# Cross-attention in rounds of one sequence, four head groups on row and column tiles of the array

## The chip, the cores and the metric

The kernel is one program on one core of a Trainium2 chip. Its engines are TensorE (PE, with its weight loads shown apart as PEld), VectorE (DVE), ScalarE (ACT) and GpSimd (POOL); SyncE (SP) issues transfers. The time is the device time of the program in microseconds, the median of several runs; lower is better. Beside it stands one profiled execution, from which every duration below is read.

## The reference, cut to what matters

The kernel computes six blocks one after the other: a cross-attention, a self-attention with rotary positions, a mixture-of-experts block, an LSTM with attention, four Mamba layers and a last expert block. The change lies in the first and its seam to the second. With 8 sequences of 32 queries, 512 context rows, 16 heads of width 8:

```python
def _L0_xattn_ref(x, y, padding_mask, Wq, bq, Wkv, bkv, qn_w, qn_b, kn_w, kn_b, Wo, bo):
    ...
    q = (x @ Wq.T + bq).reshape(b, s1, h, d)
    kv = (y @ Wkv.T + bkv).reshape(b, s2, 2, h, d)
    k, v = (kv[:, :, 0], kv[:, :, 1])
    q = _ln(q, qn_w, qn_b) * scale
    k = _ln(k, kn_w, kn_b)
    attn = jnp.einsum('bihd,bjhd->bhij', q, k)
    attn = jnp.where(padding_mask[:, None, None, :], attn, -jnp.inf)
    p = jax.nn.softmax(attn, axis=-1)
    ctx = jnp.einsum('bhij,bjhd->bihd', p, v).reshape(b, s1, c)
    out = ctx @ Wo.T + bo
    return out
...
x = x + _L0_xattn_ref(_layernorm(x, axis=-1), ctx_1024, mask_BxS2_bk0, ...)
x = x + _L0_attn_ref(_layernorm(x, axis=-1), ...)
```

## The kernel before

Each engine has its own program, and the order of work on an engine is the order in which the program is written; engines wait for one another at semaphores. All data of this stage are float32, and the compiler turns one float32 matmul into two instructions on PE.

**Projections.** Keys, queries and values of all 8 sequences are projected and the keys and queries normalised over each head (`k_proj`, `k_var`, `k_square`, `k_hat`, L325 to L357 and L500 to L524). Partition p of `kT` and of the queries holds feature p, so that 32 partitions hold a group of 4 heads. DVE spreads the queries into `qblk` (L810 to L818): for each of 16 heads one instruction multiplies all 128 partitions by a mask that leaves the 8 partitions of that head. POOL has set `qblk` to zero before (L381).

**Softmax steps.** There are 32 steps, i = 4b + g, for sequence b and group g of 4 heads. A step has 128 rows (4 heads by 32 queries) and 512 columns (context). PE: `x_scores` (L1369, one matmul over all 128 partitions of `kT`, of which the mask leaves 32 at work), into `bank[i % 2]`. DVE: `x_max` adds the mask and takes the row maximum (L839), then negates it (L841). ACT: `x_exp` (L531), which also gives the row sum. DVE: `x_norm`, the reciprocal of the sum (L847) and the multiplication by it (L850). PE: `x_transpose`, four 128x128 transposes (L1377). ACT: `x_copy_pt` copies them out of PSUM (L538). PE: `x_pv`, four matmuls with 32 columns of values as weights (L1386), output on the 32 partitions of group g. Every tile between these is double-buffered (slots i % 2 of `T`). After the four groups of a sequence DVE picks each head's own part out of the product (`x_heads`, L858 and L861).

PE's loop runs scores of step i, transposes of step i - 2, product of step i - 3. DVE's loop runs `x_max(i)`, `x_norm(i - 1)`, every fourth time `x_heads`, and in between takes maxima that a later block needs: `l_size` (L866) over the 8 parts of the context in steps 0 to 7 and over three parts of the weights `lw` at step 12. ACT runs `x_exp(i)`, `x_copy_pt(i - 2)`.

**Around the steps.** Ahead of the steps DVE computes `wmean` (L828, L829) from the self-attention's weights; POOL then subtracts it from them (L405) and scales parts of `lw` (L411). After the steps DVE reduces the maxima to `ltop` (L882, L883), POOL reduces these over partitions (L415) for a later block, and only then adds a bias for the self-attention (L418) and sets `qblk` to zero for it (L420). Meanwhile the output projection (L1399), the residual (L889) and layernorm 1 (L762 to L788) run, and the self-attention begins: PE `a_proj` (L1414), `a_var` (L1422), `a_rot` (L1429); ACT `a_square`, `a_rstd` (L553 to L560); DVE `a_z0` (L906), `a_rope` (L916, L918, L922); POOL L426; 8 turns m of these, then scores L1451, whose softmax DVE begins at L942, and the product L1473.

Of the kernel before, what the change touches and what calls it, by code (L numbers as in the profile page):

```python
# [36 lines left out]
XG = 4  # L37
# [90 lines left out]
def build(nc, arr, out, upto=99):  # L128

    with ExitStack() as ctx:  # L130
# [127 lines left out]
        def slot(n, i):  # L258
# [120 lines left out]
        def _(pool):  # L379
            step = Steps(pool, sem["pool_step"])  # L380
            pool.memset(qblk[:, :, :, :, :], 0.0).then_inc(sem["mask_ready"], 1)  # L381

            pool.wait_ge(sem["d_mask"], 16)
            pool.tensor_scalar(maskb[:, :], mask8[:, :], -MASKED, MASKED, ALU.mult, ALU.add) \
# [93 lines left out]
        def _(act):  # L478
# [47 lines left out]
            def x_exp(i):  # L526

                act.wait_ge(sem["x_max"], i + 1)
                if i >= 2:
                    act.wait_ge(sem["x_norm"], i - 1)  # L530
                act.activation(T[:, 2 + i % 2, :], T[:, i % 2, :], ACT.Exp, bias=xneg[:, i:i + 1],  # L531
                               accum_out=xz[:, i:i + 1]).then_inc(sem["x_exp"], 1)

            def x_copy_pt(i):
                act.wait_ge(sem["x_tr"], i + 1)
                if i >= 2:
                    act.wait_ge(sem["x_pv"], i - 1)
# [216 lines left out]
        def _(dve):  # L754
# [55 lines left out]
            def q_blocks(first):  # L810

                if first == 0:
                    dve.wait_ge(sem["k_done"], 1)
                    dve.wait_ge(sem["mask_ready"], 1)
                for h in (first, first + 1):
                    ins = dve.tensor_scalar(qblk[:, h // 4, :, h % 4, :], T[:, 10, 0:TOK].rearrange("p (b s) -> p b s", b=B),  # L816
                                            cst[:, C_HM16 + h:C_HM16 + h + 1], None, ALU.mult)
                ins.then_inc(sem["qblk_ready"], 1)  # L818

            for s in range(1 + B):  # L820
# [3 lines left out]
                if s >= 1:  # L824
                    q_blocks(2 * (s - 1))

            dve.wait_ge(sem["d_attn"], 32)
            step(dve.tensor_reduce(wmean[:, :], wqkv[:, 0:2 * AH * AD].rearrange("p (h d) -> p h d", d=AD), AX, ALU.add))  # L828
            dve.tensor_scalar(wmean[:, :], wmean[:, :], 1.0 / AD, None, ALU.mult).then_inc(sem["a_wmean"], 1)  # L829

            def x_max(i):

                b = i // XG
                if i == 0:
                    dve.wait_ge(sem["mask_ready"], 2)
                dve.wait_ge(sem["x_score"], i + 1)
                if i >= 2:
                    dve.wait_ge(sem["x_exp"], i - 1)
                step(dve.tensor_tensor_reduce(T[:, i % 2, :], bank[i % 2][:, :], maskb[:, b * SK:(b + 1) * SK],  # L839
                                              1.0, FLOOR, ALU.add, ALU.max, xmax[:, i:i + 1]))  # L840
                dve.tensor_scalar(xneg[:, i:i + 1], xmax[:, i:i + 1], -1.0, None, ALU.mult) \  # L841
                   .then_inc(sem["x_max"], 1)

            def x_norm(i):
# [3 lines left out]
                if i >= 2:  # L848
                    dve.wait_ge(sem["x_tr"], i - 1)
# [1070 lines left out]
```

## Time and profile before

| what | time, us |
|---|---|
| median of 3 runs | 739.34 (737.47 to 740.51) |
| the profiled execution | 740.16 |
| its span, first to last instruction | 738.3 |
| projections of the cross-attention | 13.4 to 36.8 |
| softmax steps, first scores to last `x_heads` | 40.44 to 125.2 |
| output projection and layernorm 1 | 125.3 to 130.1 |
| self-attention, 8 turns and after | 130.2 to 186.9 |
| mixture of experts, LSTM, Mamba, last block | 186.9 to 738.3 |

The first section of the profile page gives each engine's busy time, the second the busy share in 40 slices of 18.5 us (a digit is tenths; the row PEclk is the granted clock of TensorE in tenths of full speed). The other views group instructions by source line, list them in order of time, or give sums over stretches of time. A releaser behind an arrow is what ended the idle time ahead of an instruction.

### The profile page before, as it was taken

The page shows a single profiled execution, that of the slowest core. Times are in us where ns is not written, and L with a number is a line of the kernel's source. Part 1 is how long each engine was busy: PE and PEld are TensorE (multiplying, and loading weights), DVE is VectorE, ACT ScalarE, POOL GpSimd, SP SyncE. Part 2 cuts the span into 40 slices and gives each one's busy share as a digit, 9 for nine tenths or more (in the row PEclk, how much of TensorE's full clock was granted, in tenths as well). Part 3 has the DMA queues.
Part 4 walks back from the last instruction along what each step waited for, and adds up shares of the span by engine and source line. Part 5 has one row for each costly group of instructions (what it writes and reads, how often), then busy time and mean ns, then how long its engine had stood idle before and what let it go on. Part 6 is the DMA issues. An engine that isn't in the chain of part 4 may idle for free.

```text
span 738.3 us, 21781 instructions
## 1 busy us (share of the span) xinstructions
PE 618.2 (84%) x8501; PEld 476.5 (65%) x8501; DVE 498.4 (68%) x1962; ACT 306.1 (41%) x859; POOL 144.8 (20%) x177
## 2 busy tenths in 40 slices
PE   4969997876889758999899998997689888988866
PEld 3536665434678558888888888886466556655634
DVE  1697665477453467777777777774287888878883
ACT  2935453433365543333333333333445445544511
POOL 3330000420800000000000000000543564346500
PEclk9999999887799855555555555555599999999997
DMA  9700000000100200000000000000000000000000
GB/s 344 321 1 1 1 1 2 1 1 2 41 1 1 66 22 3 0 0 0 0 0 0 0 0 0 0 0 1 0 1 1 0 1 1 1 0 1 0 1 7
DMA packets 6057, 15.26 MB, mean 21 GB/s; under 512 B 2640, under 2 KB 3288, under 8 KB 5504
## 3 DMA queue, kind: packets, MB, share of 16 engines
q1 hardware_dynamic: 5296, 11.19, 4.1%
q10 hardware_dynamic: 720, 3.55, 1.2%
q8 instruction: 24, 0.39, 0.2%
q14 instruction: 17, 0.14, 0.1%
HBM read 14.60 MB, written 0.13 MB: 20 GB/s over the span
## 4 chain that ended last, share of the span: by engine, by line
PE 49%; DVE 30%; ACT 11%; issue 8%; DMA 1%; POOL 1%; DVEq 0%; SPq 0%; ACTq 0%
PE bank L1659 9%; PE bank L1732 7%; PE bank L1568 6%; PE bank L1386 4%; PE bank L1369 4%; ACT esp L661 3%; PE bank L1519 2%; DVE ssum L1122 2%; DVE T L1192 2%; ACT a L647 2%; ACT e L663 2%; PE bank L1377 2%; PE bank L1506 2%; DVE rz L1159 2%; DVE zs L1157 2%
## 5 line engine op out<-in xcount | busy, mean ns | idle before, releaser
L1568 PE MATMUL bank<-esp,qblk 128*128 128x1 f16 (+1 forms) x2048 | 66.6, 166 | 0.7 <-ACT esp L661 0.7
L1568 PE MATMUL bank<-hsp,kT 128*128 128x2 f16 x2048 | 63.6, 166 | 2.5 <-DVE hsp L1150 1.7
L1568 PEld LDWEIGHTS bank<-hsp,kT 128*128 128x128 f16 x2048 | 60.0, 104 | 3.5 <-DVE hsp L1147 1.7
L1568 PEld LDWEIGHTS bank<-esp,qblk 128*128 128x128 f16 x2048 | 61.3, 104 | 1.3 <-ACT esp L661 1.1
L647 ACT ACTIVATE a<-opre 128x4 f32<-128x4 f32 x64 | 13.1, 205 | 115.8 <-DVE opre L1110 115.8
L455 POOL MEMSET ctxT<- 128x128 f32 x1 | 0.3, 312 | 306.2 <-DVE xres L1166 306.2
L1192 DVE SCALAR_TENSOR_TENSOR T<-bank,bct,T 128x256 f32<-128x256 f32 x112 | 46.4, 475 | 1.3 <-PE bank L1745 1.3
L1179 DVE TENSOR_TENSOR_SCAN qblk<-ctxT,bank 128x512 f32<-128x512 f32 x32 | 37.6, 1208 | 13.5 <-PE bank L1732 13.1
L1568 PE MATMUL bank<-asp,lsp 128*128 128x4 f16 x768 | 30.7, 168 | 16.4 <-DVE asp L1112 16.4
L1568 PEld LDWEIGHTS bank<-asp,lsp 128*128 128x128 f16 x768 | 25.4, 105 | 27.9 <-DVE asp L1112 27.7
L1179 DVE TENSOR_TENSOR_SCAN w<-kT,bank 128x512 f32<-128x512 f32 x32 | 37.5, 1207 | 8.2 <-PE bank L1732 8.2
L531 ACT ACTIVATE T<-T,xneg 128x512 f32<-128x512 f32 x32 | 23.1, 722 | 42.1 <-DVE xneg L841 42.1
L1369 PE MATMUL bank<-kT,qblk 128*128 128x512 f32 x64 | 37.1, 668 | 3.6 <-DVE qblk L816 3.6
L655 ACT ACTIVATE gact<-bank,lgate 128x16 f32<-128x16 f32 x64 | 17.5, 274 | 45.6 <-PE bank L1568 45.6
L1732 PE MATMUL bank<-maskb,T 128*128 128x512 f32 x64 | 35.9, 685 | 0.5 <-ACT T L725 0.5
L1732 PE MATMUL bank<-w,T 128*128 128x512 f32 x64 | 34.9, 660 | 1.0 <-DVE w L1179 1.0
L839 DVE CUSTOM_DVE_ANT_0 T<-bank,maskb 128x512 f32<-128x512 f32 x32 | 22.1, 690 | 19.9 <-PE bank L1369 19.9
L1568 PE MATMUL bank<-hsp,lsp 128*128 128x4 f16 x984 | 35.4, 166 | 0.0
L1386 PE MATMUL bank<-T,vx 128*32 128x128 f32 x256 | 33.6, 276 | 0.2
L1568 PE MATMUL bank<-gx,T 128*128 (+1 forms) x198 | 27.7, 190 | 6.5 <-DVE gx L1091 6.5
L1568 PEld LDWEIGHTS bank<-hsp,lsp 128*128 128x128 f16 x984 | 32.0, 105 | 0.0
L473 POOL TENSOR_TENSOR kT<-T,aneg 128x496 f32<-128x496 f32 x32 | 31.3, 1015 | 3.3 <-DVE T L1249 3.3
(327 smaller groups left out, 1471.1 us busy)
## 6 DMA issues: line engine op xcount, KB each, us to landing
w<-in_w_dram SPq DMA_DIRECT2D x2, 2048.0 KB
ctxT<-in_ctxT_dram SPq DMA_DIRECT2D x8, 256.0 KB, 12.9
wqkv<-in_qkvT_dram ACTq DMA_DIRECT2D x1, 1536.0 KB, 11.7
w<-in_mw_dram SPq DMA_DIRECT2D x1, 1024.0 KB, 5.1
lw<-in_lw_dram SPq DMA_DIRECT2D x1, 960.0 KB, 19.8
rows<-in_rows_dram ACTq DMA_DIRECT2D x1, 772.0 KB, 7.9
wqkv<-in_fw_dram SPq DMA_DIRECT2D x1, 532.0 KB, 3.3
T<-in_mask_dram ACTq DMA_DIRECT2D x1, 512.0 KB, 5.8
```

The lines of the kernel that those rows point to most:

```text
L473: pool.tensor_tensor(tile(c, i), pat(delta, [[0, NG], [S, BT], [1, S - 1]], ch * P + 1), pat(aneg[:, :], [[1, NG], [0, BT], [0, S - 1]], ( ...
L531: act.activation(T[:, 2 + i % 2, :], T[:, i % 2, :], ACT.Exp, bias=xneg[:, i:i + 1], accum_out=xz[:, i:i + 1]).then_inc(sem["x_exp"], 1)
L647: act.activation(a32[:, g, :], opre[:, g, :], ACT.Tanh).then_inc(sem["at_32"], 1)
L661: act.activation(esp[:, g, 0, :], ssum[:, g, :], ACT.Exp, scale=lexp[:, :]) \
L839: step(dve.tensor_tensor_reduce(T[:, i % 2, :], bank[i % 2][:, :], maskb[:, b * SK:(b + 1) * SK], 1.0, FLOOR, ALU.add, ALU.max, xmax[:, i: ...
L1179: dve.tensor_tensor_scan(out=hid[q % 2][:, at], data0=decay[q % 2][:, at], data1=bank[i % 4][:, :], initial=0.0, op0=ALU.mult, op1=ALU.add ...
L1192: ins = dve.scalar_tensor_tensor(out=cacc[n % 2], in0=hT, scalar=c_n, in1=cacc[n % 2], op0=ALU.mult, op1=ALU.add)
L1369: pe.matmul(bank[i % 2][:, :], qblk[:, g, b, :, :], kT[:, b * SK:(b + 1) * SK], start=True, stop=True).then_inc(sem["x_score"], 1)
L1386: ins = pe.matmul(bank[4 + b % 2][32 * g:32 * g + 32, 0:P], vx[:, b * KC + c, 32 * g:32 * g + 32], T[:, 6 + i % 2, c * P:(c + 1) * P], sta ...
L1568: return pe.matmul(out, lhsT, rhs, start=start, stop=stop, skip_group_check=True)
L1659: return pe.matmul(out, lhsT, rhs, start=start, stop=stop, skip_group_check=True)
L1732: pe.matmul(bank[i % 4][:, :], duT[s][:, ch * P:(ch + 1) * P], diagb[s][:, ng * 512:(ng + 1) * 512], start=True, stop=True).then_inc(sem[" ...
```

## The change

**PE, rows.** The queries are spread into 4 blocks instead of 16: block h carries head h of every group, on that group's 32 partitions (`q_block`, mask `C_HM`, four instructions; the scale is now a constant with a minus sign). Scores of group g are then a matmul over the 32 partitions of the group alone, and the four groups of a sequence are issued one after the other into banks 0 to 3 (`x_scores(b)`), after all four `x_max` of the sequence before.

**PE, columns.** `x_pv(b)` runs once for a sequence, with the four groups inside the loop over the parts of the context, so that neighbouring matmuls have different output partitions. It waits for all four copies of the sequence.

**PE, order.** Round b is scores of sequence b, product of sequence b - 2, sixteen transposes of sequence b - 1.

**DVE.** The scores come out negated; so the maximum becomes a minimum that is at once the bias of the exponential, and the negation (L841) with the wait ahead of it goes. The exponential and the division are written in place; there are six slots for them (`XR`) and eight for the transposed probabilities. `wmean` is computed in round 0, after the third division. The `l_size` of the context move into the 8 turns of the self-attention, those of `lw` and the reduction to `ltop` behind these turns.

**ACT.** `x_copy_pt` runs four steps behind `x_exp`, instead of two.

**POOL.** The first zeroing of `qblk` goes. The reduction over partitions moves from ahead of the self-attention's bias to behind its 8 turns.

Semaphores of the last block are replaced by ones that exist already (`f_gate`, `f_h`), with the counts adapted.

The diff, cut to this:

```diff
-            pool.memset(qblk[:, :, :, :, :], 0.0).then_inc(sem["mask_ready"], 1)
...
-            pool.wait_ge(sem["l_stat"], 1)
-            pool.partition_all_reduce(lall[:, :], ltop[:, :], P, REDUCE.max).then_inc(sem["l_max"], 1)
-
             pool.wait_ge(sem["x_res"], 1)
             pool.tensor_tensor(xbias[:, :, :], xres[:, :, :], pat(r("projb"), [[0, NJ], [1, D]]), ALU.add) \
                 .then_inc(sem["xb_ready"], 1)
...
+
+            pool.wait_ge(sem["l_stat"], 1)
+            pool.partition_all_reduce(lall[:, :], ltop[:, :], P, REDUCE.max).then_inc(sem["l_max"], 1)
...
-                if i >= 2:
-                    act.wait_ge(sem["x_norm"], i - 1)
-                act.activation(T[:, 2 + i % 2, :], T[:, i % 2, :], ACT.Exp, bias=xneg[:, i:i + 1],
+                act.activation(x_soft(i), x_soft(i), ACT.Exp, scale=-1.0, bias=xneg[:, i:i + 1],
                                accum_out=xz[:, i:i + 1]).then_inc(sem["x_exp"], 1)
...
+            for i in range((B + 1) * XG):
                 if i < B * XG:
                     x_exp(i)
-                if i >= 2:
-                    x_copy_pt(i - 2)
+                if i >= XG:
+                    x_copy_pt(i - XG)
...
+                dve.tensor_scalar(qblk[:, 0, :, h, :], T[:, 10, 0:TOK].rearrange("p (b s) -> p b s", b=B),
+                                  cst[:, C_HM + h:C_HM + h + 1], -XD ** -0.5, ALU.mult, ALU.mult) \
+                   .then_inc(sem["qblk_ready"], 1)
...
-                step(dve.tensor_tensor_reduce(T[:, i % 2, :], bank[i % 2][:, :], maskb[:, b * SK:(b + 1) * SK],
-                                              1.0, FLOOR, ALU.add, ALU.max, xmax[:, i:i + 1]))
-                dve.tensor_scalar(xneg[:, i:i + 1], xmax[:, i:i + 1], -1.0, None, ALU.mult) \
-                   .then_inc(sem["x_max"], 1)
+                if i >= XR:
+                    dve.wait_ge(sem["x_tr"], i - XR + 1)
+                dve.tensor_tensor_reduce(x_soft(i), bank[g][:, :], maskb[:, b * SK:(b + 1) * SK],
+                                         1.0, -FLOOR, ALU.add, ALU.min, xneg[:, i:i + 1]).then_inc(sem["x_max"], 1)
...
+            for b in range(B + 2):
+                for g in range(XG):
+                    i = b * XG + g
+                    if i < B * XG:
+                        x_max(i)
+                    if 1 <= i <= B * XG:
+                        x_norm(i - 1)
+                if b == 0:
+                    dve.wait_ge(sem["d_attn"], 32)
+                    step(dve.tensor_reduce(wmean[:, :], wqkv[:, 0:2 * AH * AD].rearrange("p (h d) -> p h d", d=AD), AX, ALU.add))
+                    dve.tensor_scalar(wmean[:, :], wmean[:, :], 1.0 / AD, None, ALU.mult).then_inc(sem["a_wmean"], 1)
+                if b >= 2:
+                    x_heads(b - 2)
...
                 if m >= 1:
                     a_rope(m - 1)
+                if m < B:
+                    l_size(lmax[:, m:m + 1], ctxT[:, m * SK:(m + 1) * SK])
+            dve.wait_ge(sem["l_w"], 4)
+            for k, (at, end) in enumerate(((14, 15), (13, 14), (4, 13))):
+                l_size(lmax[:, B + k:B + k + 1], lw[:, at * D:end * D])
...
+                for g in range(XG):
+                    own = slice(32 * g, 32 * g + 32)
+                    pe.matmul(bank[g][:, :], qblk[own, 0, b, :, :], kT[own, b * SK:(b + 1) * SK],
+                              start=True, stop=True).then_inc(sem["x_score"], 1)
...
                 for c in range(KC):
-                    ins = pe.matmul(bank[4 + b % 2][32 * g:32 * g + 32, 0:P], vx[:, b * KC + c, 32 * g:32 * g + 32],
-                                    T[:, 6 + i % 2, c * P:(c + 1) * P], start=(c == 0), stop=(c == KC - 1))
+                    for g in range(XG):
+                        ins = pe.matmul(bank[6 + b % 2][32 * g:32 * g + 32, 0:P], vx[:, b * KC + c, 32 * g:32 * g + 32],
+                                        x_probT(b * XG + g)[:, c * P:(c + 1) * P], start=(c == 0), stop=(c == KC - 1))
...
+            for b in range(B + 2):
+                if b < B:
+                    x_scores(b)
+                if b >= 2:
+                    x_pv(b - 2)
+                if 1 <= b <= B:
+                    for g in range(XG):
+                        x_transpose((b - 1) * XG + g)
```

PE at the start of the softmax steps, before: scores (L1369), transposes (L1377) and products (L1386) in steps.

```order
L1369 MATMUL bank<-kT,qblk 128x512 x3
L1377 MATMUL bank<-cst,T 128x128 x4
L1369 MATMUL bank<-kT,qblk 128x512
L1377 MATMUL bank<-cst,T 128x128 x4
L1386 MATMUL bank<-T,vx 32x128 x4
```

The same place after the change, to the end of round 2:

```order
L1369 MATMUL bank<-kT,qblk 128x512 x8
L1377 MATMUL bank<-cst,T 128x128 x16
L1369 MATMUL bank<-kT,qblk 128x512 x4
L1386 MATMUL bank<-T,vx 32x128 x16
L1377 MATMUL bank<-cst,T 128x128 x16
```

The number of matmuls is the same; they now stand in fours and sixteens.

POOL from the subtraction of `wmean` on, before (the rows "ISA" without operands are set-up instructions):

```order
L405 TENSOR_TENSOR wqkv<-wqkv,wmean 128x2048
L411 TENSOR_SCALAR lw<-lw 128x128
L411 TENSOR_SCALAR lw<-lw 128x384
L411 TENSOR_SCALAR lw<-lw 128x128
L413 MEMSET expo 128x1
L415 ISA
L415 ISA lall<-ltop 128x4
L418 ISA
L418 TENSOR_TENSOR xbias<-xres,rows 128x256
L420 MEMSET qblk 128x4096
L426 TENSOR_SCALAR T<-T,vec 128x512 x8
```

And after (L434 is the reduction over partitions):

```order
L412 TENSOR_TENSOR wqkv<-wqkv,wmean 128x2048
L418 TENSOR_SCALAR lw<-lw 128x128
L418 TENSOR_SCALAR lw<-lw 128x384
L418 TENSOR_SCALAR lw<-lw 128x128
L420 MEMSET expo 128x1
L422 TENSOR_TENSOR xbias<-xres,rows 128x256
L424 MEMSET qblk 128x4096
L430 TENSOR_SCALAR T<-T,vec 128x512 x8
L434 ISA
L434 ISA lall<-ltop 128x4
```

The bias and the zeroing no longer stand behind the reduction.

## Rows read from the trace of the kernel before

**Rows 1.** Sums by stretch: us, busy time by engine (instructions), PEclk, DMA share, GB/s

```profile
80.00:100.00 20.00, 20.00 (x115) 12.85 (x114) 12.56 (x45) 10.51 (x25) 0.00 (x0) 1.00 0.00 1
```

**Rows 2.** One step in order of time, all engines: start, length, instruction [idle before]

```profile
114.60 0.15 DVE L847 RECIPROCAL xrz<-xz 128x1 f32<-128x1 f32 x1
...
114.78 0.49 DVE L850 TENSOR_SCALAR T<-T,xrz 128x512 f32<-128x512 f32 x1
...
115.11 1.13 PE L1369 MATMUL bank<-kT,qblk 128*128 128x512 f32 x2
...
116.07 0.60 PE L1377 MATMUL bank<-cst,T 128*128 128x128 f32 x4
...
116.28 0.69 DVE L839 CUSTOM_DVE_ANT_0 T<-bank,maskb 128x512 f32<-128x512 f32 x1 [1.00 <-PE bank L1369]
...
116.60 1.06 PE L1386 MATMUL bank<-T,vx 128*32 128x128 f32 x8
```

**Rows 3.** PE in order of time: products of the self-attention, two column tiles

```profile
176.41 1.97 PE L1473 MATMUL bank<-qblk,vx 128*64 128x128 f32 x32 [1.55 <-DVE qblk L963]
```

**Rows 4.** In order of time: scores of the self-attention, tiles of 64 rows by 32 columns

```profile
163.74 2.34 PE L1451 MATMUL bank<-kT 64*32 64x32 f32 x204 [1.58 <-DVE kT L922]
```

**Rows 5.** In order of time: start of the softmax steps

```profile
40.30 2.27 DVE L828 TENSOR_REDUCE wmean<-wqkv 128x32 f32<-128x2048 f32 x1
...
40.44 4.52 PE L1369 MATMUL bank<-kT,qblk 128*128 128x512 f32 x6 [3.62 <-DVE qblk L816]
...
42.87 3.62 POOL L405 TENSOR_TENSOR wqkv<-wqkv,wmean 128x2048 f32<-128x2048 f32 x1 [1.91 <-DVE wmean L829]
...
45.14 1.63 DVE L850 TENSOR_SCALAR T<-T,xrz 128x512 f32<-128x512 f32 x1
```

**Rows 6.** In order of time: end of the softmax steps, layernorm 1

```profile
124.46 0.29 DVE L858 TENSOR_TENSOR T<-bank,cst 128x128 f32<-128x128 f32 x1 [3.01 <-PE bank L1386]
124.79 0.37 DVE L861 TENSOR_REDUCE oT<-T 128x32 f32<-128x128 f32 x1
...
126.56 0.42 DVE L889 TENSOR_TENSOR xres<-xbias,bank 128x256 f32<-128x256 f32 x1 [0.87 <-PE bank L1399]
...
128.38 0.61 DVE L783 TENSOR_SCALAR xn<-xres,mv,rs 128x128 f32<-128x128 f32 x2 [0.60 <-ACT rs L491]
```

**Rows 7.** POOL in order of time, 125 to 138 us

```profile
133.16 0.71 POOL L418 TENSOR_TENSOR xbias<-xres,rows 128x256 f32<-128x256 f32 x1 [7.21 <-issue]
133.83 3.50 POOL L420 MEMSET qblk<- 128x4096 f32 x1
```

**Rows 8.** In order of time: layernorm 0 beside POOL

```profile
7.14 3.60 POOL L384 TENSOR_SCALAR maskb<-T 128x4096 bf16<-128x4096 uint8 x1 [2.89 <-DMA T<-in_mask_dram]
...
10.01 1.06 DVE L783 TENSOR_SCALAR xn<-x_in,mv,rs 128x128 f32<-128x128 f32 x2 [5.26 <-ACT rs L491]
```

**Rows 9.** DVE in order of time: a turn of the self-attention, and behind the turns

```profile
149.23 0.75 DVE L906 SCALAR_TENSOR_TENSOR T<-bank,vec,T 128x512 f32<-128x512 f32 x1 [0.83 <-ACT T L560]
...
155.46 0.75 DVE L906 SCALAR_TENSOR_TENSOR T<-bank,vec,T 128x512 f32<-128x512 f32 x1 [0.82 <-ACT T L560]
...
165.41 0.76 DVE L942 SCALAR_TENSOR_TENSOR T<-bank,cst 128x256 f32<-128x256 f32 x2 [1.72 <-PE bank L1451]
```

**Rows 10.** Groups by line, `l_size` of the context: count, busy us, mean ns, idle before

```profile
L866 DVE TENSOR_REDUCE lmax<-ctxT 128x1 f32<-128x512 f32 x8 | 5.4, 677 | 0.0
```

**Rows 11.** DVE in order of time: `l_size` of `lw`

```profile
72.96 1.73 DVE L866 TENSOR_REDUCE lmax<-lw 128x1 f32<-128x128 f32 x3
```

**Rows 12.** Sums by stretch, columns as in Rows 1, around changes of the clock

```profile
124.00:128.00 4.00, 1.14 (x8) 0.68 (x6) 2.31 (x10) 0.18 (x1) 0.39 (x1) 1.00 0.00 0
...
132.00:136.00 4.00, 4.00 (x9) 2.44 (x8) 0.00 (x0) 1.46 (x3) 2.84 (x2) 0.50 0.00 0
136.00:140.00 4.00, 2.91 (x10) 1.50 (x9) 1.69 (x3) 2.86 (x5) 2.12 (x3) 1.00 0.00 0
...
176.00:180.00 4.00, 2.41 (x36) 2.20 (x37) 3.80 (x8) 1.09 (x2) 0.00 (x0) 1.00 0.00 0
```

More of the change, by code:

```diff
@@ L535, in x_copy_pt @@
                 act.wait_ge(sem["x_tr"], i + 1)
-                if i >= 2:
-                    act.wait_ge(sem["x_pv"], i - 1)
-                act.activation(T[:, 6 + i % 2, :], bank[2 + i % 2][:, :], ACT.Copy).then_inc(sem["x_pt"], 1)
-            for i in range(B * XG + 2):
+                if i >= 2 * XG:
+                    act.wait_ge(sem["x_pv"], i // XG - 1)
+                act.activation(x_probT(i), bank[4 + i % 2][:, :], ACT.Copy).then_inc(sem["x_pt"], 1)
+            for i in range((B + 1) * XG):
                 if i < B * XG:
                     x_exp(i)
-                if i >= 2:
-                    x_copy_pt(i - 2)
+                if i >= XG:
+                    x_copy_pt(i - XG)
             ln_rstd(1)
@@ L808, in v_evac, with q_block @@
                 dve.tensor_copy(pat(vx[:, b * KC, :], [[1, SK]]), bank[4 + b % 2][:, :]).then_inc(sem["v_evac"], 1)
-            def q_blocks(first):
-                if first == 0:
+            def q_block(h):
+                if h == 0:
                     dve.wait_ge(sem["k_done"], 1)
[L814 to L818, printed above, removed]
+                dve.tensor_scalar(qblk[:, 0, :, h, :], T[:, 10, 0:TOK].rearrange("p (b s) -> p b s", b=B),
+                                  cst[:, C_HM + h:C_HM + h + 1], -XD ** -0.5, ALU.mult, ALU.mult) \
+                   .then_inc(sem["qblk_ready"], 1)
             for s in range(1 + B):
@@ L866, in l_size @@
                 step.mark(dve.tensor_reduce(to, of, AX, ALU.max, apply_absolute_value=True))
-            for i in range(B * XG + 4):
-                if i < B * XG:
-                    x_max(i)
-                if 1 <= i <= B * XG:
-                    x_norm(i - 1)
-                if i >= 4 and (i - 4) % XG == XG - 1:
-                    x_heads((i - 4) // XG)
-                if i < B:
-                    l_size(lmax[:, i:i + 1], ctxT[:, i * SK:(i + 1) * SK])
-                if i == 12:
-                    dve.wait_ge(sem["l_w"], 4)
-                    for k, (at, end) in enumerate(((14, 15), (13, 14), (4, 13))):
-                        l_size(lmax[:, B + k:B + k + 1], lw[:, at * D:end * D])
-            step.sync()
-            step(dve.tensor_reduce(ltop[:, 0:1], lmax[:, 0:B], AX, ALU.max))
-            dve.tensor_copy(ltop[:, 1:4], lmax[:, B:B + 3]).then_inc(sem["l_stat"], 1)
+            for b in range(B + 2):
[11 more added lines that the diff above has]
+                    x_heads(b - 2)
             dve.wait_ge(sem["x_oT"], B)
@@ L929, in _ @@
                     a_rope(m - 1)
+                if m < B:
[3 more added lines that the diff above has]
+                l_size(lmax[:, B + k:B + k + 1], lw[:, at * D:end * D])
+            step.sync()
+            step(dve.tensor_reduce(ltop[:, 0:1], lmax[:, 0:B], AX, ALU.max))
+            dve.tensor_copy(ltop[:, 1:4], lmax[:, B:B + 3]).then_inc(sem["l_stat"], 1)
             dve.wait_ge(sem["a_rope"], 8)
@@ L1366, in x_scores @@
                     pe.wait_ge(sem["k_rstd"], 1 + B)
-                if i >= 2:
-                    pe.wait_ge(sem["x_max"], i - 1)
-                pe.matmul(bank[i % 2][:, :], qblk[:, g, b, :, :], kT[:, b * SK:(b + 1) * SK],
-                          start=True, stop=True).then_inc(sem["x_score"], 1)
+                else:
+                    pe.wait_ge(sem["x_max"], XG * b)
+                for g in range(XG):
+                    own = slice(32 * g, 32 * g + 32)
+                    pe.matmul(bank[g][:, :], qblk[own, 0, b, :, :], kT[own, b * SK:(b + 1) * SK],
+                              start=True, stop=True).then_inc(sem["x_score"], 1)
             def x_transpose(i):
```

66 lines of the change are left out of this document (27 added, 39 removed).

## The prediction

> **What bounds the kernel now.** I read the sums by stretch first. In the middle of the softmax steps PE is busy 20.00 of 20.00 us at the full clock, DVE 12.56, ACT 10.51 [rows 1]. Then one step in order of time [rows 2]: scores begin at 115.11, transposes at 116.07, the product at 116.60, and `x_max` waits 1.00 us for the scores. The spans of 1.13, 0.60 and 1.06 us overlap at their ends. The product's 8 instructions of 128 columns start 109 ns apart, 0.85 us in all; at that pace the scores' two of 512 also stream 0.85, and the transposes' four 0.43. Two changes of form a step leave some 0.2 us each. That is 2.5 us. 32 steps from the first scores at 40.44 [rows 5] to the last `x_heads` at 125.16 [rows 6] make 84.7 us, all of it on the path, since the self-attention needs their result.
>
> DVE's own step, without waits, is the second thing to see. From its begin to the next instruction's, `x_max` takes 0.68 (116.28 with 0.69 long), the reciprocal 0.19 (114.60 to 114.78), the multiplication 0.41 of its 0.49. ACT's 10.51 us in 20 are 1.3 a step, 1.2 where its instructions follow one another closely.
>
> **The scores and the product.** *Do tiles run side by side?* For column tiles the trace shows it. The self-attention's products use two column tiles: 32 instructions of 128 columns in 1.97 us [rows 3], 62 ns each. The same length on one column tile costs 8 in 1.06 us, 109 ns apart [rows 2]. So two tiles run at once. Its scores, on 64 rows by 32 columns, start 204 instructions in 2.34 us [rows 4], 11.5 ns each, where 32 columns stream for 27 ns (a quarter of 109); so more than two tiles can be at work. Four row tiles of 32 with 512 columns are in no row. Bounds: the four scores take 4 x 0.85 = 3.4 us a round if they don't overlap, 0.85 if they do wholly. I take 0.85, by the nearest rows, 3 and 4. The Trainium skill (TensorE: Matmul & The Clock Gate, Part 3) gives 3.07x for four row tiles at 512 columns. That would make 1.1 us of the scores, and 0.26 us more in each of seven rounds, an estimate of 1.8 us by that page; no row here has the form.
>
> *PE's round* at the full clock is then 0.85 + 0.87 + 4 x 0.44 = 3.5 us of streaming and 0.6 for three changes of form, against 10 before. PE no longer bounds.
>
> *DVE's round* is what is late next: 4 x (0.68 + 0.19 + 0.41) = 5.1, and `x_heads` 0.6 [rows 6]. The negation (0.15 and its wait) is gone. Scores of the next sequence start only after the fourth `x_max` and need 1.13 us to the first result [rows 2]; one division (0.6) and `x_heads` (0.6) stand in this gap, so 0.1 to 0.4 us stays open. I followed the waits of the three programs with these durations and get **6.1 us a round**, 1.52 a step. ACT's 4 x 1.22 = 4.9 fits in.
>
> *The ends.* First scores at 40.3 (they wait for POOL's last part of `kT`, not for `qblk`); the clock there is low (three matmuls in 4.52 us [rows 5]), so the first `x_max` begins at 42.4, as before. Round 0 has `wmean`, 2.45 us with its scaling [rows 5], for which before the first scores were a cover; here the gap and the missing `x_heads` cover half: 7.3 us. Round 1 has POOL's subtraction. In the trace the multiplication at 45.14 takes 1.63 in place of 0.49 and ends as POOL's L405 does [rows 5]. Now that 3.6 us instruction begins 0.8 us ahead of the fourth division: a stall of 2.4 us, 8.1 for the round. Five more rounds of 6.0 to 6.1. From the last round's first `x_max` to the last `x_heads`: four steps (4.5), the rest of divisions and transposes, with copies one behind the other (5.3), product and heads (2.1): 11.9. Sum 42.1 + 7.3 + 8.1 + 30.3 + 11.9 = **99.7 at the full clock**.
>
> *The clock.* After 124 to 128, with PE busy 1.14 of 4.00 us, it fell from 2.4 to 1.2 GHz; in 132 to 136 PE was busy all the time at 0.50, and from 136 it had 1.00 [rows 12]. Here PE idles some 4 us after the first scores, so rounds 0 and 1 run at 1.2 GHz. There PE has 7 us of streaming and 0.6 of changes; the round comes to 7.95 us. It is then nearly always busy, which should bring 2.4 GHz back. I take two to three rounds at 7.95: **the steps end at 104**, 21.2 us sooner. Bounds are 99.7 and 114.7 (all rounds low).
>
> **What is moved.** *POOL, reduction over partitions.* POOL stood 7.21 us after it [rows 7], so bias and zeroing came at 133.16. Now both start as soon as the residual is there, 0.05 us after L889. The bias takes 0.7, the zeroing 3.5, till 4.25 us after L889; layernorm's multiplication (two instructions, 0.61) is due 1.40 us after it (128.38 against 126.98) [rows 6]. Where POOL held on, DVE's same line took 1.06 at 10.01 and ended 0.33 after POOL's L384 [rows 8], and L850 waited likewise [rows 5]. POOL read and wrote in both; whether a zeroing, which only writes, holds DVE up is in no row. Bounds 0 and 4.25 + 0.28 - 1.40 - 0.3 = **+2.9**; I take 2.9, as DVE writes too and both nearest rows show a full stop. DVE idled before L906 for 7 us while PE projected, but that wait begins behind this multiplication, so nothing covers it. The Trainium skill (SBUF — State Buffer, "Who interferes with whom") says that a GpSimd instruction and such a VectorE multiplication exclude each other for their whole length; by that rule the sum stands, and with no hold it would be 720.6. The reduction itself now runs behind the turns, where POOL idles until the self-attention ends: nothing.
>
> *`l_size`, context.* 8 x 0.68 [rows 10], 0.60 from begin to begin. Before they lay in DVE's idle time. In the turns DVE idles 0.83 of 6.2 us per two turns [rows 9]; two of them ask 1.2, so 0.4 a pair stays, and one chain is delayed at once: **+2.0** over 8 turns (bounds 0 and 4.8).
>
> *`l_size`, lw, and ltop.* 1.73 [rows 11] and 0.4, in DVE's wait of 1.72 for L1451 [rows 9]: **+0.4**. Taking ltop out of the end of the steps gives 0.2 back.
>
> *First zeroing, 12 fewer instructions for `qblk`:* nothing. POOL waits for the mask by transfer anyway [rows 8], and the projections are PE's.
>
> **Sum.** -21.2 + 2.9 + 2.0 + 0.4 - 0.2 = -16.1. The profiled execution, 740.16, becomes 724.1. The median of the runs is 0.8 lower, so 723.3; I say **723.5**.
>
> **Rivals.**
> (a) *Clock back at once, zeroing free.* Steps end at 101, and the 2.9 falls away: **717**. For it: PE's low rounds are dense. Against: rows 5 and 8.
> (b) *Low clock throughout.* With 7.6 of 7.95 us PE is not quite without a break, and once high it has only 57% to do, with four short transposes late in a round. In 176 to 180, with 2.41 of 4.00 us busy, the clock stayed up [rows 12], which speaks against. Steps end at 114.7: **734**.
> (c) *Row tiles one after the other.* Scores take 3.4 us, PE's round 6.7 plus waits, 8.1 by the same reckoning; steps end at 112 to 118: **731 to 737**. This is the change not doing what it says. For it: only column tiles are shown; against: rows 4 mix two halves of the rows.
> (d) *Slower.* (c) with the clock held low: scores 6.8, round 13.1 us, steps end at 148, 23 later than now; with the 5 us moved, **767**. It costs more than now from about 9 us a round (now 4 x 2.48 = 9.9, but the moved 5 us and the longer ends count against it). PE would be busy all the time, as in 132 to 136, after which the clock rose; hence it is unlikely.
>
> **How the numbers follow.** Forecast 0.50 (719 to 728), (a) 0.13, (b) 0.15, (c) 0.14, (d) 0.04, 0.04 for seams I don't see. The range leaves out (d), half of (a)'s lower and (c)'s upper end: 715.5 to 736. Half a percent, what a measurement can tell from no change, is 3.7 us: faster below 735.6. Chances: 0.88 faster, 0.06 the same, 0.06 slower.
>
> **What would show it.** Scores: eight instructions of 512 columns in about 1.1 us, one end; if 3.5, (c). DVE: from round 2 on begins of `x_max` 1.3 us apart, with one gap a round, and little idle time between; PE idle a third. PEclk 0.5 in the stretch 44 to 58 and 1.0 after; 0.5 throughout is (b). The fourth division near 3 us long. Layernorm 1's multiplication 3.5 us in place of 0.61, beside POOL's zeroing; 0.6 refutes it. Turns of the self-attention 3.3 us in place of 3.1. I am wrong altogether if the steps end later than 120.

## The result, and the profile after

The changed kernel takes **720.61 us** (median; runs 719.57 to 720.94) against 738.40 for the kernel before on the same chip (737.39 to 740.51). The ratio is 0.9753, with a 95% interval of 0.9726 to 0.978: faster by 2.5%, where 723.5 had been forecast in a range of 715.5 to 736. The profiled execution took 740.16 before and takes 720.94 now, with a span of 719.1.

The page of the changed kernel, its first two sections and the group of the transposes (line, engine, operation, tiles; busy us and mean ns; idle time before and its releaser):

```profile
PE 578.0 (80%) x8501; PEld 450.8 (63%) x8501; DVE 491.9 (68%) x1918; ACT 304.4 (42%) x859; POOL 139.8 (19%) x176
...
PEclk9978988978999555555555555555699999999996
...
L1377 PE MATMUL bank<-cst,T 128*128 128x128 f32 x128 | 21.0, 303 | 10.0 <-ACT T L543 9.8
```

The page hardly shows the change: it lies in the third to tenth of 40 slices. So I put the milestones of both traces beside one another (us from the span's start, or differences of such times):

| from the trace | before | after | difference |
|---|---|---|---|
| last `x_heads` ends | 125.16 | 102.24 | -22.92 |
| from there to layernorm 1's multiplication | 3.22 | 3.08 | -0.14 |
| that multiplication, two instructions | 0.61 | 3.00 | +2.39 |
| its end to the first `a_proj` | 1.22 | 1.32 | +0.10 |
| the eight turns of the self-attention | 33.47 | 34.37 | +0.90 |
| last turn to its softmax | 1.73 | 1.97 | +0.24 |
| softmax to the end of the self-attention | 21.53 | 21.29 | -0.24 |
| from there to the span's end | 551.40 | 551.86 | +0.46 |
| span | 738.34 | 719.14 | -19.2 |

Some 22.9 us came out up to the end of the softmax steps and some 3.7 were given back behind them. The last row but one is work that none of the experiments below touches; over the twelve traces of this document it takes 549.1 to 551.9 us, and this is how far chance alone moves a single trace. Sums by stretch of the changed kernel (us; busy time and instructions of PE, PEld, DVE, ACT, POOL; PEclk), to be read beside [rows 1]:

```profile
44.00:58.00 14.00, 7.54 (x32) 3.74 (x32) 12.36 (x27) 6.81 (x18) 4.84 (x5) 0.62 0.00 0
60.00:80.00 20.00, 15.39 (x184) 9.90 (x180) 17.71 (x61) 16.31 (x40) 0.00 (x0) 0.99 0.01 2
80.00:100.00 20.00, 14.53 (x164) 9.79 (x164) 14.41 (x48) 14.77 (x35) 0.00 (x0) 0.91 0.00 1
```

In 60 to 80 PE is busy 15.39 of 20 us, no longer 20.00, and DVE 17.71. DVE is the bound now. (PE's busy time still looks high because the spans of single matmuls, 273 ns for 128 columns, run on past the next one's start, 109 ns later.) The seam between two rounds, in order of time, all engines:

```profile
75.37 1.14 PE L1369 MATMUL bank<-kT,qblk 32*128 32x512 f32 x8
75.43 0.49 DVE L845 TENSOR_SCALAR T<-T,xrz 128x512 f32<-128x512 f32 x1
...
75.83 0.28 DVE L852 TENSOR_TENSOR T<-bank,cst 128x128 f32<-128x128 f32 x1
...
76.53 0.69 DVE L838 CUSTOM_DVE_ANT_0 T<-bank,maskb 128x512 f32<-128x512 f32 x1
76.91 0.81 PEld L1386 LDWEIGHTS bank<-T,vx 128*32 128x32 f32 x32 [1.23 <-ACT T L543]
76.91 1.08 PE L1386 MATMUL bank<-T,vx 128*32 128x128 f32 x32 [0.40 <-ACT T L543]
...
77.15 0.16 DVE L844 RECIPROCAL xrz<-xz 128x1 f32<-128x1 f32 x1
...
79.94 0.16 DVE L844 RECIPROCAL xrz<-xz 128x1 f32<-128x1 f32 x1 [0.30 <-ACT T L536]
```

The scores of four head groups take 1.14 us, as long as those of one group took before (1.13 [rows 2]); the products of four take 1.08 where one took 1.06. Rounds, from one sequence's first `x_max` to the next one's, are 7.00, 9.28, 6.51, 5.92, 5.91, 5.92, 5.92 us; before, four steps took 9.93.

### The profile page after: what moved, and what is told of

Read it like the earlier page. It is cut to its first block, busy times and chain, and to the rows that moved or that the text cites. A ratio compares the mean times of both kernels' runs of the same rounds, so it can differ in the third digit from the quotient of the medians.

```text
span 719.1 us, 21665 instructions
## 1 busy us (share of the span) xinstructions
PE 578.0 (80%) x8501; PEld 450.8 (63%) x8501; DVE 491.9 (68%) x1918; ACT 304.4 (42%) x859; POOL 139.8 (19%) x176
## 4 chain that ended last, share of the span: by engine, by line
PE 41%; DVE 33%; ACT 14%; issue 9%; DMA 1%; DVEq 1%; POOL 0%; SPq 0%; ACTq 0%; POOLq 0%
PE bank L1660 9%; PE bank L1733 7%; PE bank L1569 6%; ACT esp L666 3%; PE bank L1520 2%; ACT T L536 2%; DVE ssum L1121 2%; ACT a L652 2%; DVE T L1191 2%; ACT e L668 2%; PE bank L1507 2%; DVE rz L1158 2%; DVE zs L1156 2%; DVE asp L1111 2%; DVE opre L1097 2%
## 5 line engine op out<-in xcount | busy, mean ns | idle before, releaser
L660 ACT ACTIVATE gact<-bank,lgate 128x16 f32<-128x16 f32 x64 | 17.5, 274 | 45.6 <-PE bank L1569 45.6
L480 POOL TENSOR_TENSOR ctxT<-T,aneg 128x496 f32<-128x496 f32 x32 | 31.2, 1012 | 3.1 <-DVE T L1248 3.1
L1377 PE MATMUL bank<-cst,T 128*128 128x128 f32 x128 | 21.0, 303 | 10.0 <-ACT T L543 9.8
L1121 DVE TENSOR_REDUCE ssum<-bank 128x16 f32<-128x64 f32 x64 | 14.4, 225 | 18.6 <-PE bank L1569 18.6
## 6 DMA issues: line engine op xcount, KB each, us to landing
wqkv<-in_qkvT_dram ACTq DMA_DIRECT2D x1, 1536.0 KB, 11.9
```

The lines of the kernel that those rows point to most:

```text
L480: pool.tensor_tensor(tile(c, i), pat(delta, [[0, NG], [S, BT], [1, S - 1]], ch * P + 1), pat(aneg[:, :], [[1, NG], [0, BT], [0, S - 1]], ( ...
L660: act.activation(gact[:, g, :], bank[GATES[g]][:, 0:4 * BH], ACT.Tanh, scale=lgate[:, :]) \
L1121: dve.tensor_reduce(ssum[:, g, :], pat(bank[1][:, 0:1], [[1, BH * KC], [BANK, 2], [BH * KC, 2]]), mybir.AxisListType.XY, ALU.add).then_inc ...
L1377: ins = pe.transpose(bank[4 + i % 2][:, c * P:(c + 1) * P], x_soft(i)[:, c * P:(c + 1) * P], ident)
```

## Experiments

Each edit is made to the changed kernel. Ratios are to the kernel before, run beside it on the same chip. Differences to the changed kernel are between medians taken apart, of which it has two, 720.61 and 719.56 us; the trace of each run is of one execution.

**Rows undone, columns kept** (`e1_rows_undone`).

```diff
-                dve.tensor_scalar(qblk[:, 0, :, h, :], ..., cst[:, C_HM + h:C_HM + h + 1], -XD ** -0.5, ...)
+                for h in (first, first + 1):
+                    ins = dve.tensor_scalar(qblk[:, h // 4, :, h % 4, :], ..., cst[:, C_HM16 + h:C_HM16 + h + 1], -1.0, ...)
...
-                    pe.matmul(bank[g][:, :], qblk[own, 0, b, :, :], kT[own, b * SK:(b + 1) * SK],
+                    pe.matmul(bank[g][:, :], qblk[:, g, b, :, :], kT[:, b * SK:(b + 1) * SK],
```

> The changed kernel with its scores again over all 128 partitions (16 query blocks, one matmul per group); everything else as changed. Theory (tiles running side by side is what freed TensorE): the four scores of a round stream 3.4 us in place of 0.85 us, the round grows from 5.9 to about 8.1 us at the full clock, the steps end 12 to 17 us later, the time is 733 to 738 us. Rival (the gain is from fewer changes of form on TensorE and a shorter VectorE step; tiles matter little): under 724 us.

731.91 us, ratio 0.9903 (0.9887 to 0.992), just under the range expected. PE in order of time, in a middle round:

```profile
84.50 3.70 PE L1369 MATMUL bank<-kT,qblk 128*128 128x512 f32 x8
88.13 1.08 PE L1386 MATMUL bank<-T,vx 128*32 128x128 f32 x32
```

The same eight instructions of 512 columns take 3.70 us in place of 1.14. In the trace of single instructions they start 429 to 534 ns apart; in the changed kernel four start 7 ns apart and the other four 534 ns later. So four row tiles run wholly side by side, and this is worth 2.1 us a round (8.01 in place of 5.92). The steps end at 117.33 in place of 102.24, 15.1 us later and so within the 12 to 17 expected; of the 15.1, 4.1 come back behind the steps, 2.7 of them in that last part of the kernel, which the edit doesn't touch.

**Columns undone, rows kept** (`e2_cols_undone`).

```diff
-                for c in range(KC):
-                    for g in range(XG):
+                for g in range(XG):
+                    for c in range(KC):
```

> The changed kernel with only the order of the product's 16 matmuls changed: group outside, part of the context inside, so that neighbours share their output partitions. Theory: the product takes 3.4 us a round in place of 0.87 us, and it stands ahead of the transposes, so the round grows from 5.9 to about 8.6 us; the steps end 18 to 22 us later, 738 to 743 us. Rival: order does not matter, because TensorE reaches ahead to another column tile by itself: 721 us, unchanged.

729.04 us, ratio 0.9867 (0.9846 to 0.9888): between what the two theories gave. PE in order of time:

```profile
87.08 1.14 PE L1369 MATMUL bank<-kT,qblk 32*128 32x512 f32 x8
88.61 2.46 PE L1386 MATMUL bank<-T,vx 128*32 128x128 f32 x32 [0.39 <-ACT T L543]
```

The instructions and their tiles are those of the changed kernel, only their order differs, and 1.08 us became 2.46. The single starts show why it isn't the 3.4 us of one after the other: of each group of eight the last four start in pairs with the first four of the next group, 6 to 31 ns ahead of them (which start belongs to which group follows from the order of the program and the pace of 109 ns; the trace doesn't name the tile). So PE begins a second tile four instructions early, and gets no further ahead. The 32 starts take 2.19 us with never more than two tiles at work; in the changed kernel they come in fours, 7 ns apart, and take 0.81 us. The round is 7.30 us, 1.38 longer, exactly the product's growth. With a product of 3.4 us, one after the other, the eight of them would take 8 x 0.94 = 7.5 us more, and the time would be near 736.5; most of the distance to the range expected is this overlap.

**Both undone, new order kept** (`e3_both_undone`), the two edits together.

> Both undone: scores over 128 partitions and the product group by group, in the new rounds, with the new VectorE and ScalarE parts. Theory: 31 to 37 us over the changed kernel, 751 to 758 us, so slower than the kernel before, because the rounds alone give TensorE 9 us of streaming one behind the other with waits in between. Rival (rounds and the shorter VectorE step carry a good part of the gain): at or below 735 us, faster than the kernel before.

744.77 us (740.68 to 745.96), ratio 1.0084 (1.0062 to 1.0105), slower than the kernel before by 0.8%. The trace is of the quickest of the four runs, 4.1 us under the median; where the others spend these 4 us isn't shown. PE in order of time, then the sums of 80 to 100 us:

```profile
87.48 3.70 PE L1369 MATMUL bank<-kT,qblk 128*128 128x512 f32 x8
91.12 2.46 PE L1386 MATMUL bank<-T,vx 128*32 128x128 f32 x32
```

```profile
80.00:100.00 20.00, 17.95 (x117) 11.13 (x115) 12.22 (x41) 10.76 (x26) 0.00 (x0) 1.00 0.00 1
```

The round is 9.39 us: 3.47 more than in the changed kernel, and rows and columns alone gave 2.09 and 1.38, together 3.47. From first scores to last `x_heads` it takes 85.3 us, and before 84.7. A steady round is 0.54 us shorter than the four steps of before (9.39 against 9.93), but from the last round's first `x_max` to the last `x_heads` it takes 18.6 us, where the same stretch took 13.9 before. So the order in rounds, the wider buffers and the dropped negation together bring nothing over the whole of the steps; the net gain there comes from tiles that run side by side. The time is 6 us under the range expected, about what the product's overlap of two tiles spares (7.5 us by the reckoning above).

**The cost of the zeroing** (`e4_zero_after_ln`; POOL waits ahead of it until layernorm 1 has written its result).

```diff
+            pool.wait_ge(sem["ln_xn"], 2)
             pool.memset(qblk[:, :, :, :, :], 0.0).then_inc(sem["a_zero"], 1)
```

> The changed kernel with one wait added on GpSimd: the zeroing of qblk starts only after layernorm 1 has written its result. Theory (the zeroing, though it only writes, holds the multiplication of layernorm 1 up): that line falls from 3.00 to 0.61 us and the time by 2.4 us, to 718.2 us. Rival (the multiplication is slow for another reason, or the 2.4 us are covered by the low clock of the first projections): 720.6 us, unchanged.

716.24 us, ratio 0.9702 (0.9681 to 0.9722): 4.4 under the changed kernel, more than the 2.4 us that the trace shows of it. The two medians had not been taken side by side, so both kernels ran once more, on one chip.

> The changed kernel once more, beside the next one on the same chip, to part the effect of the zeroing from where the clock's changes happen to fall. Theory (the zeroing costs 2.4 us; what the earlier comparison showed beyond that, 2 us, came from the clock, which rose sooner there and did not fall again in the steps): 720.6 us within 1.5 us.

> The changed kernel with the zeroing of qblk behind layernorm 1, once more. Theory: 2.4 us under the kernel beside it, 718.2 us, with single runs from 714 to 719 by the clock. Rival (the wait saves 4.4 us by itself): 716.2 us with the kernel beside it at 720.6 us.

719.56 us (718.08 to 721.82) and 715.32 (714.93 to 718.53), ratios 0.9744 (0.972 to 0.9767) and 0.9693 (0.9667 to 0.9718). The difference of the medians is 4.2 again, that of the means 3.6: nearer the rival's 4.4 than the theory's 2.4. In order of time, with the zeroing moved:

```profile
106.06 0.60 DVE L789 TENSOR_SCALAR xn<-xres,mv,rs 128x128 f32<-128x128 f32 x2 [0.60 <-ACT rs L499]
...
106.72 3.51 POOL L425 MEMSET qblk<- 128x4096 f32 x1 [1.26 <-DVE xn L789]
```

The multiplication is back at 0.60 us: 2.4 are shown to be the zeroing's. From the last `x_heads` to the end of the self-attention the traces of this pair differ by 3.23 (64.26 and 61.03). The 0.8 beyond the multiplication goes with the clock: 0.25 ahead of the first `a_proj`, 0.4 in the turns, 0.2 behind them. Sums by stretch of the changed kernel's second run, PEclk before the last two numbers:

```profile
104.00:108.00 4.00, 0.00 (x0) 0.00 (x0) 3.33 (x7) 0.50 (x2) 3.68 (x2) 0.89 0.14 8
108.00:112.00 4.00, 2.69 (x7) 1.97 (x8) 1.07 (x3) 0.00 (x0) 0.49 (x1) 0.50 0.00 0
112.00:116.00 4.00, 4.00 (x13) 2.65 (x11) 0.00 (x0) 2.35 (x4) 0.00 (x0) 0.75 0.00 0
```

And of the kernel with the zeroing moved:

```profile
104.00:108.00 4.00, 0.80 (x5) 0.47 (x4) 2.18 (x8) 0.50 (x2) 2.00 (x2) 0.94 0.14 8
108.00:112.00 4.00, 4.00 (x11) 2.87 (x12) 0.00 (x0) 1.19 (x2) 2.23 (x1) 0.64 0.00 0
112.00:116.00 4.00, 2.70 (x9) 1.42 (x8) 2.06 (x4) 3.01 (x5) 0.69 (x1) 1.00 0.01 2
```

PE idles while DVE is held up, and the projections behind that begin at 1.2 GHz (0.50) in the one and come back to 2.4 sooner in the other. The last 1 us of the 4.2 is in no row that I can name: runs of one kernel differ by 3.7 us, and go with the mean clock (718.08 at 0.749, 721.82 at 0.737, the same kernel), and the last part of the kernel, which no experiment touches, ranges over 2.8 us in the traces, so it may be chance. It stays open. That the clock stayed up in the steps, which the theory named for the rest, isn't needed for it: in this pair it fell in both (93.5 to 100.3 and 93.8 to 100.7).

**`wmean` ahead of the steps** (`e5_wmean_first`; reduction and scaling moved from round 0 to before the first `x_max`).

```diff
+            dve.wait_ge(sem["d_attn"], 32)
+            step(dve.tensor_reduce(wmean[:, :], ...))
+            dve.tensor_scalar(wmean[:, :], wmean[:, :], 1.0 / AD, None, ALU.mult).then_inc(sem["a_wmean"], 1)
...
-                if b == 0:
-                    dve.wait_ge(sem["d_attn"], 32)
-                    step(dve.tensor_reduce(wmean[:, :], ...))
-                    ...
```

> The changed kernel with wmean computed ahead of the first x_max again, where VectorE waits 3 us for scores. Theory: 2.3 us leave round 0 (of which up to 0.6 come back as a gap before the scores of the next round), and GpSimd's subtraction starts 8 us sooner and holds one division up by 1.5 us in place of 2.8; steps 3 to 4 us shorter, time 717 us. Rival (wmean was covered by TensorE at its low clock in round 0): 720.6 us.

717.77 us, ratio 0.9699 (0.9668 to 0.973). DVE in order of time; the reduction fills the wait for the first scores again, and POOL's subtraction, which it releases, now holds up an earlier division (1.75 us in place of 0.49):

```profile
39.72 2.27 DVE L831 TENSOR_REDUCE wmean<-wqkv 128x32 f32<-128x2048 f32 x1
...
42.65 0.69 DVE L842 CUSTOM_DVE_ANT_0 T<-bank,maskb 128x512 f32<-128x512 f32 x1 [0.45 <-PE bank L1369]
...
44.43 1.75 DVE L849 TENSOR_SCALAR T<-T,xrz 128x512 f32<-128x512 f32 x1
...
50.16 0.69 DVE L842 CUSTOM_DVE_ANT_0 T<-bank,maskb 128x512 f32<-128x512 f32 x1 [1.56 <-PE bank L1369]
```

The steps are 2.1 us shorter, not the 3 to 4 expected, and the rival was half right. Round 0 isn't shorter at all (7.51 in place of 7.00): the held-up division stands in it now, and where `wmean` had been, DVE waits 1.56 us for scores that PE delivers at 1.2 GHz. The gain is in rounds 1 and 2 (6.48 and 6.12 in place of 9.28 and 6.51).

**The subtraction behind the divisions** (`e9_sub_after_norms`).

```diff
+            pool.wait_ge(sem["x_norm"], B * XG)
             pool.tensor_tensor(wqk, wqk, pat(wmean[:, :], [[1, 2 * AH], [0, AD]]), ALU.subtract) \
```

> The changed kernel with one wait added on GpSimd: the subtraction of wmean from the weights starts only after the last of the 32 divisions. Theory (the division of 3.27 us in round 1 is held up by this subtraction): all 32 divisions take 0.49 us, the steps are 2.8 us shorter, and with no long idle time of TensorE in round 1 the clock may rise one round sooner (up to 1.5 us more); 716 to 718 us. Rival (VectorE's stall is covered by TensorE's low clock): 720.6 us.

716.80 us, ratio 0.969 (0.9662 to 0.9717), as expected. All 32 divisions take 0.49 us. The same place, where in the changed kernel the fourth division takes 3.27:

```profile
48.91 0.68 DVE L839 CUSTOM_DVE_ANT_0 T<-bank,maskb 128x512 f32<-128x512 f32 x1
...
49.71 0.49 DVE L846 TENSOR_SCALAR T<-T,xrz 128x512 f32<-128x512 f32 x1
50.12 0.68 DVE L839 CUSTOM_DVE_ANT_0 T<-bank,maskb 128x512 f32<-128x512 f32 x1
```

Round 1 is 6.47 us in place of 9.28, the stall's 2.8 us.

**`l_size` back in the steps** (`e6_lsize_in_steps`; the eight of the context after the divisions of steps 0 to 7, those of `lw` at step 12, `ltop` behind the steps).

```diff
+                    if i < B:
+                        l_size(lmax[:, i:i + 1], ctxT[:, i * SK:(i + 1) * SK])
+                    if i == 12:
+                        dve.wait_ge(sem["l_w"], 4)
+                        ...
...
-                if m < B:
-                    l_size(lmax[:, m:m + 1], ctxT[:, m * SK:(m + 1) * SK])
```

> The changed kernel with the l_size maxima and their reduction back in the softmax steps, as the kernel before had them. Theory (VectorE bounds the steps, and the turns of the self-attention had almost room for them): steps 6.5 us longer, turns and what follows 1.1 us shorter, time 726 us. Rival (VectorE has as much idle time in the steps as in the turns): 720 us or less.

723.99 us, ratio 0.9791 (0.9765 to 0.9817): 3.4 slower than the changed kernel, where 5.4 had been expected. DVE in order of time, round 0:

```profile
45.16 0.68 DVE L860 TENSOR_REDUCE lmax<-ctxT 128x1 f32<-128x512 f32 x1
45.76 0.68 DVE L838 CUSTOM_DVE_ANT_0 T<-bank,maskb 128x512 f32<-128x512 f32 x1
```

They stand on DVE's path, and the first six rounds sum to 45.6 us in place of 40.5. The turns are 33.46 us without them, 33.47 before. This move was right: a place that was free while PE bounded the steps isn't any more.

**All seams mended** (`e8_all_moved`): the edits of `e4`, `e5` and `e9`, and the context's `l_size` moved on to the projections.

```diff
                 if s < B:
                     v_evac(s)
+                    l_size(lmax[:, s:s + 1], ctxT[:, s * SK:(s + 1) * SK])
```

> A version that takes every stall found: zeroing of qblk behind layernorm 1, wmean ahead of the first x_max, subtraction behind the last division, and the l_size of the context in the projections (VectorE idles there since 12 instructions for qblk are gone), those of lw behind the turns as before. Expected from the parts: 2.4 (zeroing), 2 (wmean), 2.8 (subtraction), 0.9 (turns), some 8 us together, 712 us; up to 2 us less if the clock rises sooner. If the stalls cover one another it ends at 715 us or above.

**711.16 us** (710.21 to 712.52), ratio 0.9625 (0.9597 to 0.9653), which beats both kernels. Sums by stretch:

```profile
44.00:58.00 14.00, 9.30 (x76) 5.50 (x76) 11.20 (x38) 9.97 (x27) 0.00 (x0) 0.74 0.00 1
60.00:80.00 20.00, 15.36 (x211) 10.07 (x208) 18.46 (x63) 16.24 (x40) 0.00 (x0) 1.00 0.01 2
```

In 44 to 58 us PE ran 76 matmuls, where the changed kernel ran 32. The steps end at 96.11 and the self-attention at 157.45, 9.8 us before the changed kernel's, and the median is 9.4 lower, where some 8 had been expected. The clock didn't fall in the end of the steps in this trace, which is worth 1.5 us (below) and may be chance. The maxima in the projections had no run of their own; without them the turns are 0.91 us shorter (26.55 us in place of 27.46 from the first L897, the start of their DVE work, to their end).

## Why the prediction was right, point by point

**The bound and its successor: right.** PE bounded the steps, DVE does now. The steady round was put at 6.1 and is 5.92, in part by luck. `x_max` was booked at 0.68 us, begin to begin, where its row gives 0.69 as its length; the next instruction begins 0.61 or 0.62 later (76.53 to 77.15 above, and so in the kernel before, 116.28 to 116.89). That makes a round 0.3 shorter. The open gap of 0.1 to 0.4 was put down to the wait for the next scores, which is 0.01; it is the wait of one reciprocal for its exponential (79.94 above), and costs 0.39, of which 0.30 are idle. Four steps of 1.21, 0.70 for `x_heads` and 0.39 are the 5.92.

**Side by side: right, by an inference that the rows didn't prove.** Four row tiles, which no row of before showed, were taken as wholly parallel from [rows 3] and [rows 4], and are: 1.14 us for eight instructions. The Trainium skill (TensorE: Matmul & The Clock Gate, Part 3) gives 3.07x for four row tiles at 512 columns; from first start to last end it is 3.2x here (3.70 us with the rows undone, 1.14 with them), and the starts, 7 ns apart, show all four at work. Rival (c), tiles one after the other, was priced at 8.1 us a round and 731 to 737. The experiment with the rows undone made it true: 8.01 us and 731.91. Its price was right, its condition wasn't.

**The ends.** The first `x_max` was said to begin at 42.4, as before, and stands in the sum as 42.1; it begins at 41.92, and before at 42.73. Round 0 was put at 7.3 and is 7.00. The stall in round 1 was put at 2.4 and is 2.8. The changed kernel in order of time:

```profile
39.83 2.03 PE L1369 MATMUL bank<-kT,qblk 32*128 32x512 f32 x8 [3.28 <-POOL kT L400]
...
46.51 2.28 DVE L871 TENSOR_REDUCE wmean<-wqkv 128x32 f32<-128x2048 f32 x1
...
49.09 3.62 POOL L412 TENSOR_TENSOR wqkv<-wqkv,wmean 128x2048 f32<-128x2048 f32 x1 [8.67 <-DVE wmean L872]
...
49.72 3.27 DVE L845 TENSOR_SCALAR T<-T,xrz 128x512 f32<-128x512 f32 x1
```

The division ends 0.28 us after POOL's subtraction does, as it did in [rows 5]. What follows the last round's first `x_max` was put at 11.9 and took 13.9; with the clock high throughout, in `e8_all_moved`, it took 12.4.

**The clock: less was lost, and elsewhere.** The low clock was expected in two to three rounds from the start, for 4.3 us. It came in three pieces: 39.9 to 50.2, 53.6 to 60.4 behind the stall, and 94.6 to 98.0. Sums by stretch of the changed kernel:

```profile
40.00:50.00 10.00, 5.80 (x24) 2.36 (x23) 7.63 (x20) 3.50 (x9) 1.33 (x2) 0.50 0.00 1
50.00:54.00 4.00, 0.67 (x5) 0.42 (x4) 3.96 (x5) 1.31 (x4) 3.93 (x5) 0.93 0.00 0
54.00:60.00 6.00, 4.93 (x45) 2.64 (x45) 4.30 (x14) 4.16 (x11) 0.00 (x0) 0.50 0.00 0
94.00:98.00 4.00, 3.34 (x39) 2.84 (x40) 1.49 (x5) 0.93 (x4) 0.00 (x0) 0.57 0.00 0
```

Round 0 didn't suffer, since `wmean` hid the slow scores; round 1 did, by some 0.8 (9.28, less the 8.1 forecast at the full clock and the 0.4 by which the stall is longer), round 2 by some 0.6 (6.51 in place of 5.92), and the end by some 1.5: together 2.9. The 4.3 fits what two to three rounds of 7.95 lose against rounds of 6.1. But rounds 0 and 1 had been put at 7.3 and 8.1 already, by DVE's own delays, so that PE's 7.95 could add 0.65 to the one and nothing to the other; the sum then counts the same time twice. This is the step of the prediction that was mis-sized most. The third piece isn't in every run: it was there in six of the eight traces with tiles both ways at work, and in two not (`e4`, `e8`). It isn't fixed by the program either: `e4` and `e11` are one kernel, and the clock stayed up in the one (the end takes 12.38 us) and fell in the other (14.52). PE had been busy 3.03 and 2.10 of 4.00 us in the two stretches ahead of it in the changed kernel, 3.48 and 1.44 in `e4` with the zeroing moved, where the clock stayed up; so these rows don't say what decides. In four other traces the end took 14.5 us, 0.7 more still, with a low stretch of 6.8 us in place of 3.4. Rivals (a), clock back at once, and (b), low throughout, both fell. The steps end at 102.24, where 104 was forecast.

**The zeroing: right.** It was the least certain term, since only GpSimd instructions that also read stood in the rows. In order of time:

```profile
104.01 0.72 POOL L422 TENSOR_TENSOR xbias<-xres,rows 128x256 f32<-128x256 f32 x1 [50.08 <-DVE xres L880]
...
104.67 3.51 POOL L424 MEMSET qblk<- 128x4096 f32 x1
...
105.32 3.00 DVE L788 TENSOR_SCALAR xn<-xres,mv,rs 128x128 f32<-128x128 f32 x2 [0.60 <-ACT rs L498]
108.38 0.29 PEld L1312 LDWEIGHTS bank<-cst,xn 128*128 128x128 f32 x2 [5.18 <-DVE xn L788]
```

POOL's bias and zeroing end at 108.18 and DVE's multiplication at 108.33. With the zeroing out of its way it takes 0.60. The term is +2.4, put at +2.9. The zeroing ends 4.26 us after L880, as put (4.25), but the sum took off 0.3 for the multiplication's own length, which is 0.61, and let it run on for 0.28 behind POOL, where it runs on for 0.15; it also adds up to 2.8 and not 2.9. With 0.61 the rows would have given 2.5. The Trainium skill (SBUF — State Buffer, "Who interferes with whom") has the two exclude each other for an instruction's whole length; a zeroing that only writes does so here too, 3.00 us against 0.60.

**`l_size` in the turns: mechanism right, size wrong.** Put at +2.0, measured +0.9. The step that failed is "one chain is delayed at once". DVE in order of time, where the last turns pass into the softmax:

```profile
137.49 0.69 DVE L913 TENSOR_TENSOR kT<-T 128x512 f32<-128x512 f32 x1
138.09 0.68 DVE L860 TENSOR_REDUCE lmax<-ctxT 128x1 f32<-128x512 f32 x1
138.69 0.74 DVE L897 SCALAR_TENSOR_TENSOR T<-bank,vec,T 128x512 f32<-128x512 f32 x1
...
143.94 1.73 DVE L860 TENSOR_REDUCE lmax<-lw 128x1 f32<-128x128 f32 x3
...
145.99 0.76 DVE L941 SCALAR_TENSOR_TENSOR T<-bank,cst 128x256 f32<-128x256 f32 x2
```

No chain is delayed: the maximum fills DVE's wait ahead of L897, which was 0.82 in every second turn [rows 9], and two turns take 6.50 us in place of 6.23, +0.27 a pair. DVE's instructions now follow one another closely there, so it has become what bounds the turns. From the first L897 to the end of the turns it is 27.46 us in all nine traces with the eight maxima there, and 26.55 or 26.56 in the three without, so the 0.9 isn't the clock's. The part of `lw` and `ltop` was put at +0.4 and is +0.24, taking `ltop` out at -0.2 and is -0.14.

**The sum** was -16.1 and is -19.2. Of the 3.1 us, 1.7 lie in the steps (a steady round 0.15 shorter, and less lost to the clock, with the end 0.5 longer even at the full clock), 1.1 in the turns, 0.5 in the zeroing, and -0.2 in the rest.

## What to carry to other kernels

Put matmuls on separate tiles next to one another in the program: here the same 32 instructions on four column tiles took 1.08 us with the tile in the inner loop and 2.46 in the outer, where only two tiles overlapped. For row tiles no run tried the other order. Once the bounding engine has been relieved, every piece of work that was hidden in its shadow has to be placed anew; here mending four such seams gave 9.4 us, half of what the change had gained; 1.5 of the 9.4 may be the clock's chance. Before GpSimd work is moved or unblocked, look at which VectorE multiplication stands beside it for the time that the GpSimd instruction lasts.

## What the runs showed of the hardware

- A GpSimd zeroing, which reads nothing, holds a VectorE multiplication by a per-partition scalar up just as a subtraction does (3.00 us in place of 0.60).
- Four row tiles of 32 rows in float32 at 512 columns run wholly in parallel (eight instructions in 1.14 us, 3.70 on the whole array).
- With column tiles in blocks of eight instructions each, never more than two tiles were at work (32 starts in 2.19 us, 0.81 when interleaved); the second tile began 6 to 31 ns behind the fifth to eighth instruction of the first.
- The clock can fall in the middle of a stage, 94.6 to 98.0 us, with PE busy 2.10 of the 4.00 us ahead, and not do so in `e4` with 1.44 of 4.00 there. It fell in `e11` and not in `e4`, which are one kernel. The price is some 1.5 to 2.1 us here.
